# Post-norm attention and ternary FFN layer: the first row's first quad of scores moved ahead by a step, and where raw FFN weights wait

## The chip, the cores and the metric

The kernel runs on one core of a Trainium2 chip. The metric is device time in microseconds (us) of one execution. Three runs of the kernel before gave 1080.48, 1075.93 and 1077.56 us; their median is 1077.56 us.

## The reference

For 16 rows (batch entries) of 512 tokens and 256 features, in float32:

```
qkv = x @ Wqkv + bqkv                      # 16 heads of 16 features
scores = q . k / 16, keys of the own block of 128 tokens and of the two beside it
attn = softmax(where(|kpos - qpos| <= 128, scores, -1e30))
x1 = layernorm(x + (attn @ v) @ Wout + bout)
gamma = mean(|W|);  Wq = clip(round(W / (gamma + 1e-5)), -1, 1)     # for W1 and W2
out = layernorm(x1 + relu(x1 @ Wq1.T + b1) @ Wq2.T + b2)
```

The layer norms have no gain or shift. So the FFN weights have to be brought to -1, 0 or 1 on the chip, with thresholds that need the mean of all their absolute values.

## The kernel before, in words

**Tiling.** The 16 heads are taken in four quads of four heads (v or vq = 0 to 3). A quad's scores and its maxima are each worked out in 12 units: i = 0 to 11, head i // 3, and u = i % 3 says which key blocks (or query blocks). Two units of every three are one matmul of 384 columns, the third is two matmuls of 256 columns (`BLOCKS`, `PCOL`). Products that need float32 accuracy are done from a high and a low part ("hi" and "lo"), which for queries and keys are stacked along the partitions in `q_stack` and `k_stack` by DMAs.

**One quad's chain.** `max_scores` (TensorE, L567) fills a PSUM bank `mx`; `row_max` (VectorE, L1061) adds the band and takes the maximum; `neg_max` (L1069, L1072) negates the 16 maxima and splits them in two; step "nmt" transposes them (TensorE, L631; ScalarE copies them out, L938), and SP's DMA `maxima` (L489) writes them as two more rows of `q_stack`. Then `scores` (TensorE, L549) fills a bank `st` with scores that already have their maximum subtracted, `exp` (ScalarE, L895) turns them into `probs`, `mask` (GpSimd, L1285 and L1289; two per quad, after exp unit 5 and 11) zeroes what lies outside the band, and step "pv" (TensorE, L641) multiplies them by the values. There are two `st` and two `mx` banks: a score unit waits for the exponential of the unit two before it, a max unit for the row maximum of the unit two before it.

**Order.** Every engine runs its own instruction list in order. `steps` calls the body for at = -2, -1, 0, ... 16. At step `at`, row `at` has its attention, row at - 1 its FFN, and rows at + 1 and at + 2 are prepared. Each step has four parts v = 0 to 3, each a list `SIDE[v]` of side work, into which `WOVEN[v]` puts 12 score units and 12 max units. The scores are those of quad v of this row, the maxima those two quads ahead (`max_quad`): quads 2 and 3 of this row, then quads 0 and 1 of the next. At at = -1 there are no scores; `first_maxima` puts quad 0's maxima in v = 2 (among the projection "vp") and quad 1's maxima in v = 3: units 0 and 1 at "xr", then the transpose "nmt" of quad 0's maxima, then units 2 to 11 at "pv". In step 0, part v = 0 has no other work of TensorE than the "nmt" of quad 1, quad 0's scores and quad 2's maxima, since row 0 has no row before it. Part v = 1 begins with the projection "qk" (0) of row 1 (L592).

**SP's queue.** `TRANSFERS` is the order in which SP issues, in each step, the stack DMAs of a quad (six, L449), the `maxima` DMA after part v's "nmt", the columns of x, the residual x (into `y`, L482) and the stores. SP waits in that order. At at = -1 the order comes to: x, stack 0, stack 1, maxima (3) (which is quad 0's), stack 2; stack 3 follows as the first of step 0. `scores` of quad 0 waits for quad 0's maxima in `q_stack` and for stack 2.

**Raw weights.** The FFN weights come in raw and are quantised by GpSimd (`quantise`, L1299, L1300, L1303) in eight chunks of 512 columns. Chunks 0 to 3 (W2) and 4 and 5 (half of W1) lie in the second half of `probs`, which quad 1's exponentials will overwrite, chunks 6 and 7 in `x1`. The comparison "below" goes through the tile `oT_x1T_lo`. Chunks 0 to 2 are quantised at at = -1 (`other_weights`), 3 to 5 at the head of step 0 ahead of quad 0's masks, 6 and 7 after the two masks of quad 1. The first exponential of quad 1 waits for six chunks, and the first "ot" and "x1" on ScalarE and VectorE and the first "f1" on TensorE for all eight.

Of the kernel before, what the change touches and what calls it, by code (L numbers as in the profile page):

```python
# [27 lines left out]
B, S, D = 16, 512, 256  # L28
H, DH, W = 16, 16, 128
FF = 1024  # L30
NB = S // W
KC = D // P
# [42 lines left out]

TRANSFERS = (('stack', 3), ('maxima', 0), ('x', 0), ('stack', 0), ('maxima', 1), ('stack', 1), ('residual', 0), ('maxima', 2), ('maxima', 3), ('stack', 2), ('store', 0), ('store', 1))

LAG = {"ln1": 3, "ln2": 0, "qk": 0, "ut": 0, "ot": 1, "x1t": 0, "f1": 0, "op": 0, "f2": 0}
N_PAIRS = 2
WARM_END = {"ut": 3, "ot": 4, "op": 6, "x1t": 12}  # L80
# [67 lines left out]
def first_maxima(v):  # L148

    steps = {2: [(("f1", 1), range(N_MAX)), ("vp", range(N_MAX, UNITS))], 3: [("xr", range(N_MAX)), ("pv", range(N_MAX, UNITS))]}  # L150
    units = dict(steps.get(v, []))
    return [[(2 * u, "max", u) for u in units.get(s, ())] for s in SIDE[v]]


def stages(at):
# [67 lines left out]
def postln_layer(nc, xT, x, wqkv, bqk, bv, wout, bout, w1T, b1, w2T, b2, out):  # L223
    ctx = ExitStack()
    with ctx:
# [65 lines left out]
        WQRAW = PRF[0][:, 0:KC * 3 * D].rearrange("p (c n) -> p c n", c=KC)  # L291
        W2RAW = PRF[1][:, 0:FC * D]
        WORAW = PRF[1][:, FC * D:FC * D + KC * D]
        W1RAW = [X1[:, :, :].rearrange(FLAT), PRF[1][:, FC * D + KC * D:FC * D + KC * D + FF]]
        B1RAW = O[:, 0:2, :].rearrange(FLAT)


        def chunk(n):

            if n < 4:  # L300
                return W2RAW[:, S * n:S * n + S], W2Q[:, 2 * n:2 * n + 2, :].rearrange(FLAT), 1
            k, at = int(n < CHUNKS_IN_PROBS), S * (n % 2)
            return W1RAW[k][:, at:at + S], W1Q[:, k, at:at + S], 0

        CHUNKS, CHUNKS_IN_PROBS = 8, 6

        s_wq = sem("wqkv_in")
        s_w1 = sem("w1_in")
# [105 lines left out]
        @block.sync  # L414
        def _(sp):

            sp.dma_start(WQRAW, wqkv.rearrange("(c p) n -> p c n", p=P)).then_inc(s_wq, 16)

            def more_weights():
                sp.dma_start(WORAW.rearrange("p (c n) -> p c n", c=KC), wout.rearrange("(c p) n -> p c n", p=P)) \  # L420
                    .then_inc(s_wo, 16)
                sp.dma_start(W2RAW.rearrange("p (c n) -> p c n", n=D), w2T.rearrange("(c p) n -> p c n", p=P)) \
                    .then_inc(s_w2, 16)
                for k in range(KC):
                    sp.dma_start(W1RAW[k], w1T[P * k:P * k + P]).then_inc(s_w1, 16)
                sp.wait_ge(s_const, CONSTANTS)
                for row in (0, 32, 64, 96):
                    blocks = b1.rearrange("(c i n) -> i c n", i=2, n=P)[row // 64:row // 64 + 1]
                    sp.dma_start(B1RAW[row:row + 1].rearrange("a (c n) -> a c n", n=P), blocks).then_inc(s_b1, 16)
                sp.dma_start(BOUT[:, :], bout[None, :].to_broadcast([P, D])).then_inc(s_b2, 16)  # L430
                sp.dma_start(B2[:, :], b2[None, :].to_broadcast([P, D])).then_inc(s_b2, 16)

            def stack(r, v, first):


                c, ih = v // 2, v % 2
                if not first:
                    sp.wait_ge(s_stf, 12 * (4 * r - 4 + v) + 12)
                half = slice(64 * ih, 64 * ih + 64)
                heads = slice(4 * ih, 4 * ih + 4)  # L440
                for part, done in ((0, s_qkh), (1, s_qkl)):
                    sp.wait_ge(done, 4 * r + 2 * c + 2)
                    for dst, j, terms in ((SQ, 2 * c, (0, 1, 0)), (SK, 2 * c + 1, (0, 0, 1))):
                        if first and v == 0 and dst is SK:
                            continue
                        for t in range(3):
                            if terms[t] == part:
                                rows = slice(64 * c + 16 * t, 64 * c + 16 * t + 16)
                                sp.dma_start(dst[rows, heads, :].bitcast(F32), QK[j][part][half, :].bitcast(F32)) \  # L449
                                    .then_inc(s_stk[v], 16)  # L450

            def step(b, at):
                attn, post, nxt, nxt2 = stages(at)
                for kind, v in TRANSFERS:
                    if kind == "x" and nxt2:
                        x_columns(b + 2)
                        if at == -2:
                            sp.dma_start(BQK[:, :], bqk).then_inc(s_small, 16)
                            sp.dma_start(BV[:, :], bv).then_inc(s_small, 16)
                            more_weights()  # L460
                    elif kind == "stack" and v == 3 and attn:
                        stack(b, 3, at == 0)
                    elif kind == "stack" and v < 3 and nxt:
                        stack(b + 1, v, at == -1)
                    elif kind == "store" and post:
                        store(b, v, slice(2 * v, 2 * v + 2) if at == B else slice(v, v + 3, 2))
                    elif kind == "residual" and attn:
                        residual(b)
                    elif kind == "maxima" and row_of(v, "nmt", at) is not None:
                        dr, vq = row_of(v, "nmt", at)  # L470
                        maxima(b + dr, vq)

            def x_columns(r):
                if r > 0:
                    sp.wait_ge(s_xl, r)
                sp.dma_start(XRAW[:, :, :], xT[r:r + 1].rearrange("a (c p) t -> p (a c) t", p=P)).then_inc(s_x, 16)

            def residual(r):
                if r > 0:
                    for t in range(TB):  # L480
                        sp.wait_ge(*x1_done(r - 1, t))
                sp.dma_start(Y[:, :, :], x[r:r + 1].rearrange("a (t p) d -> p (a t) d", p=P)).then_inc(s_xr, 16)  # L482

            def maxima(r, vq):

                q, c, ih = 4 * r + vq, vq // 2, vq % 2
                sp.wait_ge(s_nmt, q + 1)
                rows = SQ[64 * c + 48:64 * c + 50, 4 * ih:4 * ih + 4, :].bitcast(F32)
                sp.dma_start(rows.rearrange("a g (n q) -> a (g n) q", n=NB), NMT[:, vq % 2].bitcast(F32)) \  # L489
                    .then_inc(s_nmin[vq], 16)  # L490

            def store(b, h, tiles):
                sp.wait_ge(s_o, 4 * (b - 1) + 2 * h + 2)
                sp.dma_start(out[b - 1:b].rearrange("a (t p) d -> p (a t) d", p=P)[:, tiles, :],
                             X1[:, tiles, :]).then_inc(s_out, 16)

            steps(step)
            sp.wait_ge(s_out, 32 * B)


        @block.tensor
        def _(pe):
# [238 lines left out]
            def step(b, at):  # L741
                attn = stages(at)[0]
                for v in range(QUADS):
                    q = max_quad(v, at)
                    for step, woven in zip(SIDE[v], first_maxima(v) if at == -1 else WOVEN[v]):
                        places = [0]

                        def units(until):
                            for place, kind, i in woven:
                                if places[0] <= place < until:  # L750
                                    if kind == "scores" and attn:
                                        scores(b, v, i, at)
                                    elif kind == "max" and q is not None:
                                        max_scores(b + q[0], q[1], i, at == -1)
# [97 lines left out]
        def _(act):  # L852
# [45 lines left out]
            def side_work(v, step, b, dr, vq, at):  # L898
# [47 lines left out]
                    act.activation(U[:, :], PG[:, 2 * k, :], ACT.Identity).then_inc(s_u, 1)  # L946
                elif name == "ot":
                    act.wait_ge(s_otf, 2 * r + 2)
                    if first:
                        act.wait_ge(s_quant, CHUNKS)  # L950
                    else:
                        act.wait_ge(s_f1f, FC * r)
                    for i in range(KC):
                        act.activation(OT[0][:, i, :], PG[:, 2 * k + i, :], ACT.Identity, bias=BV[:, i:i + 1]) \
# [23 lines left out]
            def step(b, at):  # L978
                attn = stages(at)[0]
                for v in range(QUADS):  # L980
# [3 lines left out]
                    for step, woven in zip(SIDE[v], WOVEN[v]):  # L984
# [2 lines left out]
                        if row is not None and before:  # L987
                            side_work(v, step, b, *row, at)
                        for _, kind, i in woven:
                            if kind == "scores" and attn:  # L990
                                exp(b, v, i, at)
                        if row is not None and not before:
                            side_work(v, step, b, *row, at)
                if at == B:
# [31 lines left out]
        def _(dve):  # L1026
# [48 lines left out]
            def side_work(v, step, b, dr, vq, at):  # L1075
# [26 lines left out]
                        on = dve.tensor_tensor(o, ut[:, i, :, :, 0:DH], sums.to_broadcast([P, TB, 2, DH]), ALU.mult)  # L1102
                    on.then_inc(s_on, 1)
                elif name == "ot":
                    if first:
                        dve.wait_ge(s_quant, CHUNKS)
                    for i in range(KC):
                        dve.wait_ge(s_oth, 2 * r + i + 1)
                        dve.scalar_tensor_tensor(OT[1][:, i, :], PG[:, 2 * k + i, :], BV[:, i:i + 1],
# [146 lines left out]
        def _(pool):  # L1256
# [36 lines left out]
            def quantise(n):  # L1293

                raw, ternary, i = chunk(n)
                if n > 1:
                    pool.wait_ge(s_quant, n - 1)
                below = OT[1][:, n % 2, :]
                pool.tensor_scalar(below, raw, THR[:, 2 + i:3 + i], None, ALU.is_lt).then_inc(s_below, 1)  # L1299
                pool.tensor_scalar(ternary, raw, THR[:, i:i + 1], None, ALU.is_gt).then_inc(s_above, 1)  # L1300
                pool.wait_ge(s_below, n + 1)
# [3 lines left out]
            def other_weights():  # L1305
# [10 lines left out]
                                       ALU.subtract).then_inc(s_b1l, 1)  # L1316
                pool.wait_ge(s_b1l, 2)
                pool.wait_ge(s_thr, 1)
                for n in range(3):
                    quantise(n)  # L1320

            quantised = [CHUNKS_IN_PROBS]


            def v_in_place(r, v, first):
# [48 lines left out]
            def step(b, at):  # L1374
                attn = stages(at)[0]
                for v in range(QUADS):
                    if at == -1 and v == 0:
                        other_weights()
                    if v == 0 and attn:
                        for vq in range(3):  # L1380
                            v_in_place(b, vq, at == 0)
                        if at == 0:
                            for n in range(3, CHUNKS_IN_PROBS):
                                quantise(n)
                    for step, woven in zip(SIDE[v], WOVEN[v]):
                        if attn:
                            for _, kind, i in woven:
                                if kind == "scores" and i in (5, 11):
                                    mask(b, v, i // 3)
                                    if at == 0 and v > 0 and quantised[0] < CHUNKS:  # L1390
                                        quantise(quantised[0])
                                        quantised[0] += 1
                            if v == 0 and step == "pv":
# [61 lines left out]
```

## Time and profile before

| | |
|---|---|
| median of 3 runs | 1077.56 us |
| the profiled execution | 1080.47 us |
| its span, first to last instruction | 1078.7 us |
| TensorE, VectorE busy | 92%, 78% |
| ScalarE, GpSimd busy | 57%, 53% |
| mean granted clock of TensorE | 0.969 |

Busy shares are of the span. Each row of the batch takes some 60 us, all alike from row 1 on; what the change touches lies in the first 110 us. PE is TensorE's matmuls, PEld its weight loads, DVE VectorE, ACT ScalarE, POOL GpSimd, SP the engine that issues most DMAs. PEclk 1.00 is 2.4 GHz and 0.50 is 1.2 GHz. Unit numbers are not in the trace; they are counted from the order of the instructions.

### The profile page before, as it was taken

Reading aid. Unit: us, or ns where it says so; the run is one execution under the profiler, and the core shown is the slowest. Engines: PE = TensorE matmul, PEld = TensorE weight load, DVE = VectorE, ACT = ScalarE, POOL = GpSimd, SP = SyncE. Lnnn points to the kernel's source line nnn. Section 1 sums busy time; section 2 is a strip of 40 time slices with the busy share of each in tenths; the row PEclk is TensorE's granted clock in tenths of the full one; section 3 lists DMA queues with packets and bytes.
Section 4 is the critical chain, followed back from the end, with each engine's and each line's share of the span. In section 5 each row is a group of like instructions: output and inputs, shape, how many; then the busy total and the mean of one; then the engine's idle time right before and its main releaser. Section 6 shows DMA issues by size and latency. Waiting matters only on the chain.

```text
span 1078.7 us, 29877 instructions
## 1 busy us (share of the span) xinstructions
PE 996.8 (92%) x11270; PEld 782.0 (72%) x11270; DVE 845.2 (78%) x2966; ACT 620.2 (57%) x1273; POOL 570.2 (53%) x913
## 2 busy tenths in 40 slices
PE   6898999999999999999999999999999999999897
PEld 5675777777777777777767777786777778687677
DVE  3775888879788887978888787988878798887535
ACT  4244665746566574756657474765747475564632
POOL 3975356374655537465554646454464645445352
PEclk8577999999999999999999999999999999999999
DMA  9554336546354545626454652645365364435000
GB/s 222 64 82 72 57 57 95 81 74 94 55 91 66 96 70 81 99 43 97 66 96 63 94 87 49 100 65 96 56 100 80 57 96 68 73 52 81 22 21 20
DMA packets 57023, 81.90 MB, mean 76 GB/s; under 512 B 7712, under 2 KB 27696, under 8 KB 56880
## 3 DMA queue, kind: packets, MB, share of 16 engines
q1 hardware_dynamic: 56640, 79.60, 46.8%
q8 instruction: 90, 1.47, 0.7%
q10 hardware_dynamic: 240, 0.39, 0.3%
q14 instruction: 53, 0.43, 0.2%
HBM read 20.20 MB, written 8.39 MB: 26 GB/s over the span
## 4 chain that ended last, share of the span: by engine, by line
PE 61%; DVE 13%; ACT 12%; issue 6%; POOL 4%; DMA 2%; SPq 1%; DVEq 0%; POOLq 0%; ACTq 0%
PE shared L592 26%; PE shared L641 11%; PE st L549 8%; PE mx L567 6%; DVE mx L1061 6%; ACT probs L895 4%; PE shared L521 2%; ACT x L963 2%; ACT u L946 2%; DVE hid_lo L1147 2%; PE shared L654 2%; ACT oT_x1T_hi L969 2%; PE shared L612 1%; POOL probs L1285 1%; POOL probs L1289 1%
## 5 line engine op out<-in xcount | busy, mean ns | idle before, releaser
L1061 DVE CUSTOM_DVE_ANT_0 mx<-mx,band 128x384 f32<-128x384 f32 (+1 forms) x1024 | 478.9, 518 | 150.5 <-PE mx L567 145.4
L895 ACT ACTIVATE probs<-st 128x384 f32<-128x384 f32 (+1 forms) x768 | 365.1, 526 | 169.8 <-PE st L549 168.1
L1285 POOL TENSOR_SCALAR_AFFINE_SELECT probs<-probs 128x512 f32<-128x512 f32 (+1 forms) x256 | 127.8, 524 | 407.0 <-ACT probs L895 407.0
L567 PE MATMUL mx<-k_stack,q_stack 48*128 48x384 f32 (+1 forms) x1024 | 271.7, 347 | 8.5 <-DMA q_stack<-qk_lo 4.9
L549 PE MATMUL st<-q_stack,k_stack 50*128 50x384 f32 (+1 forms) x1024 | 245.1, 334 | 7.8 <-ACT probs L895 3.8
L549 PEld LDWEIGHTS st<-q_stack,k_stack 50*128 50x128 f32 x1024 | 167.7, 189 | 58.9 <-issue 29.8
L567 PEld LDWEIGHTS mx<-k_stack,q_stack 48*128 48x128 f32 x1024 | 171.8, 193 | 31.1 <-DVE rmax L1061 19.2
L641 PE MATMUL shared<-probs,v_aug 128*32 128x384 f32 (+1 forms) x2048 | 164.2, 444 | 9.4 <-POOL probs L1289 7.2
L1061 DVE DVE_READ_ACCUMULATOR2_ANT rmax<- 128x1 f32 x1024 | 144.9, 141 | 0.0
L592 PE MATMUL shared<-w2q,hid_hi 64*128 64x256 f32 x960 | 137.0, 289 | 0.0
L641 PEld LDWEIGHTS shared<-probs,v_aug 128*32 128x32 f32 x2048 | 90.5, 111 | 55.8 <-issue 17.7
L592 PE MATMUL shared<-w2q,hid_lo 64*128 64x256 f32 x960 | 129.2, 278 | 0.0
L1289 POOL TENSOR_SCALAR_AFFINE_SELECT probs<-probs 128x512 f32<-128x512 f32 (+1 forms) x256 | 127.7, 523 | 0.0
L592 PEld LDWEIGHTS shared<-w2q,hid_lo 64*128 64x128 f32 x960 | 114.9, 185 | 0.0
L592 PEld LDWEIGHTS shared<-w2q,hid_hi 64*128 64x128 f32 x960 | 113.3, 185 | 0.4
L592 PE MATMUL shared<-oT_x1T_hi,w1q 64*128 64x512 f32 x480 | 104.0, 398 | 0.0
L592 PE MATMUL shared<-oT_x1T_lo,w1q 64*128 64x512 f32 x480 | 102.4, 394 | 0.0
L946 ACT ACTIVATE u<-shared 128x512 f32<-128x512 f32 x64 | 37.9, 593 | 102.1 <-PE shared L641 102.0
L521 PE MATMUL shared<-wqkv_hi 64*128 64x512 f32 x516 | 86.6, 417 | 3.9 <-DVE qk_lo L1088 3.8
L1147 DVE SCALAR_TENSOR_TENSOR hid_lo<-shared,hid_hi 128x512 fp32r<-128x512 f32 x120 | 77.0, 682 | 16.1 <-ACT hid_hi L976 16.1
L1371 POOL TENSOR_SCALAR x<-x,ln_mv,ln_rstd 128x256 f32<-128x256 f32 x60 | 73.5, 1230 | 3.2
L976 ACT ACTIVATE hid_hi<-shared 128x512 fp32r<-128x512 f32 x120 | 65.2, 596 | 13.9 <-PE shared L592 12.7
(165 smaller groups left out, 1935.7 us busy)
## 6 DMA issues: line engine op xcount, KB each, us to landing
q_stack<-qk_hi SPq DMA_DIRECT2D x128, 128.0 KB, 4.0
k_stack<-qk_hi SPq DMA_DIRECT2D x126, 128.0 KB, 4.9
x_raw<-in_xT SPq DMA_DIRECT2D x16, 512.0 KB, 6.0
q_stack<-qk_lo SPq DMA_DIRECT2D x64, 128.0 KB, 5.6
y<-in_x SPq DMA_DIRECT2D x16, 512.0 KB, 6.3
out<-x SPq DMA_DIRECT2D x32, 256.0 KB, 2.4
k_stack<-qk_lo SPq DMA_DIRECT2D x63, 128.0 KB, 5.8
probs<-in_w2T SPq DMA_DIRECT2D x1, 1024.0 KB, 7.5
```

The lines of the kernel that those rows point to most:

```text
L521: pe.matmul(out[i][:, 0:width], WQKV[0][rows, 0, 0:P], WQKV[0][rows, 1, 0:width], start=True, stop=True)
L549: mm = pe.matmul(PST[i % N_SCORE][:, col:col + n], SK[rows, hd, W * m:W * m + W], SQ[rows, hd, q0:q0 + n], start=True, stop=True)
L567: mm = pe.matmul(PMX[i % N_MAX][:, col:col + n], SQ[rows, hd, W * m:W * m + W], SK[rows, hd, k0:k0 + n], start=True, stop=True)
L592: mm = pe.matmul(out[k][:, cols], lhs(rows), rhs(rows), start=(swap == 0 and n == 0 and bias is None), stop=(swap == 1 and n == count - 1) ...
L641: mm = pe.matmul(out[0][32 * g:32 * g + 32, q0:q0 + width], VAUG[:, vq, m, g, :], PR[:, vq % 2, g // 2, lo:lo + width], start=(m == 0), st ...
L895: act.activation(PR[:, v % 2, g // 2, lo:lo + n], PST[i % N_SCORE][:, 0:n], ACT.Exp, scale=SCALE) \
L976: act.activation(HID[0][:, f, :], PG[:, 2 * k + i, :], ACT.Relu).then_inc(s_hh, 1)
L1061: mx = dve.tensor_tensor_reduce(ps, ps, band, 1.0, -3e38, ALU.add, ALU.max, RMAX[:, g, m:m + 1])
L1147: dve.scalar_tensor_tensor(HID[1][:, f, :], PG[:, 2 * k + i, :], 0.0, HID[0][:, f, :].bitcast(F32), ALU.max, ALU.subtract).then_inc(s_hl, 1)
L1285: pool.affine_select(out=pr_before, in_=pr_before, compare_op=ALU.is_ge, fill=0.0, base=0, pattern=[[0, n], [1, W]], channel_multiplier=-1)
L1289: last = pool.affine_select(out=pr_after, in_=pr_after, compare_op=ALU.is_ge, fill=0.0, base=0, pattern=[[0, n], [-1, W]], channel_multipl ...
L1371: pool.tensor_scalar(X1[:, t, :], X1[:, t, :], MV2[:, t, 0:1], RS2[:, t:t + 1], ALU.subtract, ALU.mult).then_inc(s_o, 1)
```

## The change

- At at = -1, part v = 3, two of quad 0's score units are issued on TensorE ahead of each of quad 1's max units 6 to 11. ScalarE does the 12 exponentials right after it has copied out quad 0's maxima. In step 0, part v = 0 no scores and exponentials are left, only quad 2's maxima.
- SP issues at at = -1 the DMAs of stack 2 ahead of quad 0's maxima (`FIRST_TRANSFERS`).
- Raw chunks 4 and 5 come into `y`. The first residual DMA waits for six quantised chunks. "below" goes through `hid_lo`, and two waits for all chunks at the first "ot" go.
- The chunks are quantised otherwise: 0 to 2 as before; none at the head of step 0; 3 after quad 0's second mask, 4 and 5 after quad 1's two masks, 6 and 7 after quad 2's two masks. The first exponential of quad 1 waits for four chunks.

```diff
+FIRST_TRANSFERS = TRANSFERS[:8] + (('stack', 2),) + TRANSFERS[8:9] + TRANSFERS[10:]
...
-    return [[(2 * u, "max", u) for u in units.get(s, ())] for s in SIDE[v]]
+    def with_scores(u):
+        early = range(2 * (u - UNITS // 2), 2 * (u - UNITS // 2) + 2) if v == 3 and 2 * u >= UNITS else ()
+        return [(2 * u, "scores", i) for i in early] + [(2 * u, "max", u)]
+
+    return [sum((with_scores(u) for u in units.get(s, ())), []) for s in SIDE[v]]
...
-        W1RAW = [X1[:, :, :].rearrange(FLAT), PRF[1][:, FC * D + KC * D:FC * D + KC * D + FF]]
+        W1RAW = [X1[:, :, :].rearrange(FLAT), Y[:, :, :].rearrange(FLAT)]
...
-        CHUNKS, CHUNKS_IN_PROBS = 8, 6
+        FIRST_CHUNKS, CHUNKS_IN_PROBS, CHUNKS_IN_Y, CHUNKS = 3, 4, 6, 8
...
             def residual(r):
-                if r > 0:
+                if r == 0:
+                    sp.wait_ge(s_quant, CHUNKS_IN_Y)
+                else:
...
-                                    if kind == "scores" and attn:
+                                    if kind == "scores" and at == -1:
+                                        scores(b + 1, 0, i, at + 1)
+                                    elif kind == "scores" and attn and (at, v) != (0, 0):
                                         scores(b, v, i, at)
...
+                        if at == -1 and v == 3 and step == "nmt":
+                            for i in range(UNITS):
+                                exp(b + 1, 0, i, at + 1)
...
-                below = OT[1][:, n % 2, :]
+                below = HID[1][:, n % 2, :]
...
-                        if at == 0:
-                            for n in range(3, CHUNKS_IN_PROBS):
-                                quantise(n)
...
-                                    if at == 0 and v > 0 and quantised[0] < CHUNKS:
+                                    if at == 0 and (v, i) != (0, 5) and quantised[0] < CHUNKS:
```

## Rows read from the trace of the kernel before

**Rows 1.** The page: busy time, and the chain that ended last.
```profile
PE 996.8 (92%) x11270; PEld 782.0 (72%) x11270; DVE 845.2 (78%) x2966; ACT 620.2 (57%) x1273; POOL 570.2 (53%) x913
...
PE 61%; DVE 13%; ACT 12%; issue 6%; POOL 4%; DMA 2%; SPq 1%; DVEq 0%; POOLq 0%; ACTq 0%
```

**Rows 2.** Stretches: busy per engine (instructions), TensorE's clock, DMA share, GB/s.
```profile
core 0: us, PE busy (x) PEld busy (x) DVE busy (x) ACT busy (x) POOL busy (x), PEclk, DMA share, GB/s
36.60:46.90 10.30, 8.30 (x21) 4.32 (x20) 9.06 (x34) 1.54 (x4) 10.15 (x10) 0.50 0.63 83
46.90:49.70 2.80, 1.56 (x6) 0.81 (x6) 0.35 (x3) 0.44 (x2) 2.65 (x3) 0.50 1.13 111
49.70:58.80 9.10, 8.56 (x37) 6.15 (x37) 7.96 (x32) 5.86 (x12) 8.80 (x8) 0.50 0.76 109
```

**Rows 3.** Timeline of VectorE: start, duration, instruction [idle before <- releaser].
```profile
42.23 0.57 DVE L1061 CUSTOM_DVE_ANT_0 mx<-mx,band 128x384 f32<-128x384 f32 x1
...
47.13 0.18 DVE L1072 SCALAR_TENSOR_TENSOR neg_max<-rmax,neg_max 128x16 f32<-128x16 f32 x1
49.70 0.57 DVE L1061 CUSTOM_DVE_ANT_0 mx<-mx,band 128x384 f32<-128x384 f32 x1 [2.39 <-PE mx L567]
```

**Rows 4.** Timeline of SP's DMA issues, and landing times of q_stack's DMAs, 36 to 52.
```profile
38.72 0.66 SPq L489 DMA_DIRECT2D q_stack<-neg_maxT  x1
...
42.58 0.60 SPq L449 DMA_DIRECT2D k_stack<-qk_lo  x1
...
76.92 0.59 SPq L482 DMA_DIRECT2D y<-in_x  x1
...
DMA to landing us min/median/max: 3.3/6.1/8.8
```

**Rows 5.** Timeline of TensorE.
```profile
37.78 0.61 PE L631 MATMUL shared<-identity,neg_max 128*32 128x128 f32 x2 [0.82 <-DVE neg_max L1072]
38.35 1.20 PE L567 MATMUL mx<-k_stack,q_stack 48*128 48x256 f32 x3
...
47.36 0.63 PE L631 MATMUL shared<-identity,neg_max 128*32 128x128 f32 x2 [0.53 <-DVE neg_max L1072]
48.77 0.66 PE L549 MATMUL st<-q_stack,k_stack 50*128 50x384 f32 x1 [0.78 <-DMA k_stack<-qk_lo]
...
50.07 0.58 PE L549 MATMUL st<-q_stack,k_stack 50*128 50x256 f32 x1 [0.20 <-ACT probs L895]
51.55 0.69 PE L549 MATMUL st<-q_stack,k_stack 50*128 50x384 f32 x1
...
52.81 0.69 PE L549 MATMUL st<-q_stack,k_stack 50*128 50x384 f32 x1
...
57.32 0.76 PE L592 MATMUL shared<-xT_hi,wqkv_hi 64*128 64x512 f32 x1
```

**Rows 6.** Stretches by TensorE's clock, columns as in Rows 2.
```profile
30.00:32.00 2.00, 2.00 (x17) 1.83 (x15) 1.51 (x9) 0.00 (x0) 1.85 (x2) 0.50 0.00 0
...
62.00:64.00 2.00, 2.00 (x26) 1.47 (x26) 0.17 (x2) 0.71 (x2) 0.47 (x2) 0.87 0.00 0
```

**Rows 7.** Timeline of GpSimd.
```profile
68.55 1.00 POOL L1285 TENSOR_SCALAR_AFFINE_SELECT probs<-probs 128x512 f32<-128x512 f32 x2 [6.08 <-ACT probs L895]
...
70.48 1.57 POOL L1299 TENSOR_SCALAR oT_x1T_lo<-x,abs_sums_thresholds 128x512 fp32r<-128x512 f32 x1
...
74.97 1.00 POOL L1285 TENSOR_SCALAR_AFFINE_SELECT probs<-probs 128x512 f32<-128x512 f32 x2
...
82.07 1.00 POOL L1285 TENSOR_SCALAR_AFFINE_SELECT probs<-probs 128x512 f32<-128x512 f32 x2 [0.62 <-ACT probs L895]
...
88.29 1.00 POOL L1285 TENSOR_SCALAR_AFFINE_SELECT probs<-probs 128x512 f32<-128x512 f32 x2 [4.27 <-ACT probs L895]
```

**Rows 8.** Timeline of TensorE: the products of quads 1 and 2 with the values.
```profile
84.35 2.32 PE L641 MATMUL shared<-probs,v_aug 128*32 128x256 f32 x29
...
92.15 4.47 PE L641 MATMUL shared<-probs,v_aug 128*32 128x256 f32 x29
```

More of the change, by code:

```diff
@@ L301, in chunk @@
                 return W2RAW[:, S * n:S * n + S], W2Q[:, 2 * n:2 * n + 2, :].rearrange(FLAT), 1
-            k, at = int(n < CHUNKS_IN_PROBS), S * (n % 2)
+            k, at = int(n < CHUNKS_IN_Y), S * (n % 2)
             return W1RAW[k][:, at:at + S], W1Q[:, k, at:at + S], 0
-        CHUNKS, CHUNKS_IN_PROBS = 8, 6
+        FIRST_CHUNKS, CHUNKS_IN_PROBS, CHUNKS_IN_Y, CHUNKS = 3, 4, 6, 8
         s_wq = sem("wqkv_in")
@@ L453, in step @@
                 attn, post, nxt, nxt2 = stages(at)
-                for kind, v in TRANSFERS:
+                for kind, v in FIRST_TRANSFERS if at == -1 else TRANSFERS:
                     if kind == "x" and nxt2:
@@ L948, in side_work @@
                     act.wait_ge(s_otf, 2 * r + 2)
-                    if first:
-                        act.wait_ge(s_quant, CHUNKS)
-                    else:
+                    if not first:
                         act.wait_ge(s_f1f, FC * r)
@@ L989, in step @@
                         for _, kind, i in woven:
-                            if kind == "scores" and attn:
+                            if kind == "scores" and attn and (at, v) != (0, 0):
                                 exp(b, v, i, at)
+                        if at == -1 and v == 3 and step == "nmt":
+                            for i in range(UNITS):
+                                exp(b + 1, 0, i, at + 1)
                         if row is not None and not before:
@@ L1104, in side_work @@
                 elif name == "ot":
-                    if first:
-                        dve.wait_ge(s_quant, CHUNKS)
                     for i in range(KC):
@@ L1318, in other_weights @@
                 pool.wait_ge(s_thr, 1)
-                for n in range(3):
+                for n in range(FIRST_CHUNKS):
                     quantise(n)
-            quantised = [CHUNKS_IN_PROBS]
+            quantised = [FIRST_CHUNKS]
             def v_in_place(r, v, first):
```

## The prediction
> **What bounds the kernel now.** I read the page first: TensorE is busy 92% of the span and holds 61% of the chain that ended last [rows 1]. All that the change touches happens once, in the first 110 us; the other fifteen rows run the same lists as before and are only pushed earlier or later. So the question is when step 0 hands TensorE over to row 1's projection "qk" (0), the first work that does not depend on quads 0 to 2. Before, that was at 57.32 us [rows 5].
>
> Then I cut the time around the change into stretches [rows 2]. From 36.6 to 46.9 quad 1's maxima run, and VectorE is busy 9.06 of 10.3 us: this stretch is VectorE's. From 49.7 to 58.8 quad 0's scores and quad 2's maxima run together, TensorE busy 8.56 and VectorE 7.96 of 9.1 us: the two are nearly level. Between them VectorE stands still 2.39 us [rows 3]. The timeline of TensorE shows what it waits for: the transpose at 47.36 is out, and the first score at 48.77 is released by the last DMA of stack 2 [rows 5], issued at 42.58 behind quad 0's maxima [rows 4].
>
> **The change, part by part.**
>
> *The wait for stack 2 goes.* Its DMAs are issued some 15 us earlier. What comes next is the way through the transpose: at 37.78 a transpose of the same kind was followed by a max unit 0.57 us later [rows 5]. From 47.36 that gives a max unit at 47.93; with 0.66 us for one matmul of 384 columns [rows 5] VectorE starts at 48.6 and not at 49.70. Gain 1.1 us.
>
> *Quad 0's scores go into the second half of quad 1's maxima.* They need quad 0's maxima in `q_stack`. That DMA is issued at 38.72 [rows 4]; its landing is not in the trace. The shortest landing of the larger DMAs into the same tile at that time is 3.3 us, the longest 8.8 (on a crowded queue, which this DMA no longer meets); the lower bound is the end of its issue, 0.66. I take 3.3, the row of an empty queue: the scores can start at 42.0. Unit 6 of the maxima, behind which the first half ends, was taken by VectorE at 42.23 [rows 3], so TensorE got to it at about 41.5, and 0.5 us are lost at once. With a landing below 2.8 us nothing is lost.
>
> Two banks hold the scores, so a unit starts when the exponential two before it is done. In the stretch with the same clock a unit of 2 x 256 columns took its bank from 50.07 to 51.55, 1.48 us, and one of 384 from 51.55 to 52.81, 1.26 us [rows 5]. Bank 0 has units 0, 2, 4, 6, 8, 10, and units 2 and 8 are of 2 x 256: unit 10 starts 3 x 1.26 + 2 x 1.48 = 6.7 us after unit 0, at 48.7; unit 11 some 0.35 later, max unit 11 after it at 49.5, and VectorE ends it at 50.9. The lower bound is TensorE's own rate: 24 units in 8.56 us busy [rows 2] are 0.36 us each, and 12 score and 6 max units from 41.5 are then done at 47.9; that leaves the maxima some 1.4 us late. Before, VectorE ended them at 46.9. So the six max units take 4.0 us longer (1.4 to 4.0, more if the DMA lands later). I take 4.0, since a wait for the exponential shows between the scores of the nearest row.
>
> *Quad 2's maxima are left alone in step 0.* It is tempting to count the 12 removed score units (12 x 0.36 = 4.3 us of TensorE) as a gain. But VectorE has the same 16 reductions and accumulator reads to do, and in quad 1's stretch, without scores beside it, it needed 10.3 us with its first units early, that is the same pace: 9.1 us for quad 2 with the scores [rows 2]. I take the gain as 0; the bound below is 9.1 - 7.96 = 1.1 us, VectorE's idle time in the stretch. ScalarE's exponentials (5.86 us busy [rows 2]) bind neither there nor in their new place.
>
> So quad 2's maxima end 4.0 - 1.1 = 2.9 us later, and so does the start of "qk" (0): 57.3 becomes 60.2.
>
> *The clock.* The clock was 0.50, 1.2 GHz, until about 62.5 (0.87 in the stretch from 62 to 64 [rows 6]), after some 5 us of dense projection. If it rises at the same time, the 2.9 us of dense work that is still to do runs at twice the pace and costs half, and the delay is 1.45 us. If it rises as much later as the projection starts later, the delay stays 2.9. I take the middle, 2.2 us.
>
> A row of the trace and the Trainium skill differ on this clock. In the stretch from 30 to 32, as in those around it, TensorE was busy 2.00 of 2 us with projection and maxima, and the clock stayed at 0.50 [rows 6]. The page "TensorE: Matmul & The Clock Gate", section "Part 1: The HAM clock gate", has sustained matmul activity release the throttle. By that rule the fuller stretch after the change could bring the clock up before 50; by the row, a full busy time is not enough for it. I follow the row; the rule's outcome is the second rival.
>
> *GpSimd.* One quantisation is 4.5 us (70.48 to 74.97), two masks 1.93 us (68.55 to 70.48) [rows 7]. Before, three quantisations stood ahead of quad 0's masks; now its masks come first, and chunk 3 after them. Quad 0's masks were ready before TensorE asked for them, so this gains nothing; chunk 3 ends about 57, ahead of quad 1's exponentials. Later the chain is fuller. With everything 2.9 us late: quad 1's first masks 71.4 to 73.4, chunk 4 to 77.9, second masks to 79.9, chunk 5 to 84.4, quad 2's first masks (before at 82.07 [rows 7], so due at 85.0) to 86.9, chunk 6 to 91.4, second masks (before at 88.29, due at 91.2) to 93.3. TensorE asks for them at about 92.0 + 2.9 = 94.9 [rows 8]. So it costs 0, with 1.6 us of cover, and what hides it is the wait of the masks for the exponentials. If the cover is gone, the cost is at most one quantisation less the cover, 4.5 - 1.6 = 2.9 us. Chunk 7, the low part of row 2's columns and the biased residual come behind, and are asked for by steps of row 1.
>
> *The new wait on SP.* The residual DMA waits for six chunks, until 84.4, and was issued at 76.92 [rows 4]. Behind it on SP stands the `maxima` DMA of quad 3, issued at 85 or later before; 0 us, with under a us of cover plus the 2.9 us by which that one is late as well.
>
> *Edits of one answer.* Other tiles for raw chunks and "below" cost 0: same instructions, same sizes. The two waits that go at "ot" were met long before; 0.
>
> Sum: +4.0 - 1.1 + 0 - 0.7 (clock) = +2.2 us. The profiled execution took 1080.47 us (span 1078.7), so one like it would take 1082.7. It stands 2.9 us above the median of the three runs, and I predict against that median: 1077.56 + 2.2 = 1079.8 us.
>
> **The rivals.**
>
> A: *the overlap works as meant* (18%). The maxima land early and TensorE packs the 18 units at its own rate: +1.4 - 1.1, and quad 2's maxima lose some of their 1.1 us of idle time. With the clock's halving this is -0.5 to -1: about 1077 us. For it: TensorE has 2 of 10.3 us free in that stretch. Against it: two banks only.
>
> B: *the clock comes up early, or falls less often* (15%). If it is up before 50, "qk" (0) from 57.3 to 63.2 takes 3 us and not 5.9, and quad 2's maxima 8 us and not 9.1: +2.9 - 2.9 - 1.1 = about -1; and later, quad 2's product with the values took 4.47 us at the low clock where quad 1's took 2.32 [rows 8], and quad 3's took as long: another 2 to 4.3 us if those stretches run at 2.4 GHz. Time 1072 to 1076; the middle is 1074. The same dice can fall the other way: one more low stretch costs 2 us.
>
> C: *the quantisations get in the masks' way* (15%). GpSimd's chain has quad 2's second masks behind chunks 4, 5 and 6. From the point where they end after 94.9, TensorE waits for them at the product with the values, in order, with scores and maxima of the next part behind it. Price 2.9 us on top of 2.2, and with the first masks of quad 3 late behind chunk 7 up to 2 more: 1082.7 to 1084.7. For it: GpSimd has no gap left from 71 to 86. Against it: the exponentials bind by my sum.
>
> D: *the change does nothing that shows* (in the forecast's range): the wait moves from one DMA to another.
>
> **How the numbers follow.** Forecast 52%, A 18%, B 15%, C 15%. No change is told from a change here by 0.5%, 5.4 us: below 1072.2 or above 1082.9. Faster by that: the far end of B, 7%. Slower by that: most of C and late landings of quad 0's maxima, 13%. Same: 80%. The range for 8 in 10 goes from 1074.5 (the middle of B, and the spread of the runs before, 4.5 us) to 1084.5 (C).
>
> **What would show it.** Right: VectorE's gap at the change from quad 1's to quad 2's maxima under 1.8 us; quad 1's last max at 50 to 51; a stall of TensorE for quad 0's maxima of about 0.5 us; quad 2's stretch 9 us without scores; "qk" (0) at about 60. Wrong: a projection that starts before 58; TensorE's product of quad 2 released by GpSimd; a clock of 1.00 before 58. The prediction fails if row 1 starts earlier than before at the same clock.

## The result

The changed kernel took 1084.09 us (median of 9 runs, 1082.45 to 1084.97) and the kernel before, in the same rounds, 1080.48 us (9 runs, 1075.93 to 1081.51). The ratio is 1.0042, with a 95% interval of 1.0028 to 1.0056: the change costs 3 to 6 us, around 4.5. I had forecast 1079.8 us, +2.2 us on a base of 1077.56. The direction was right, and the size was half of the 4.5 us.

The changed kernel's profiled execution took 1083.39 us, 2.9 us more than that of before. On the page the busy times and the chain have hardly moved (TensorE 996.8 before, [rows 1]), so the time went into waiting:

```profile
span 1081.6 us, 29875 instructions
...
PE 997.2 (92%) x11270; PEld 781.2 (72%) x11270; DVE 845.3 (78%) x2966; ACT 619.6 (57%) x1273; POOL 568.7 (53%) x913
...
PE 61%; DVE 14%; ACT 11%; issue 6%; POOL 4%; DMA 2%; SPq 1%; DVEq 0%; POOLq 0%; ACTq 0%
```

The three stretches that answer to [rows 2] are quad 1's maxima, now with quad 0's scores, the gap, and quad 2's maxima, now alone. Columns as there.

```profile
37.30:51.40 14.10, 12.67 (x37) 8.08 (x37) 9.25 (x34) 7.55 (x16) 10.95 (x14) 0.50 0.44 59
51.40:53.80 2.40, 1.32 (x4) 0.68 (x4) 0.96 (x3) 0.27 (x1) 2.40 (x5) 0.50 0.00 0
53.80:63.00 9.20, 7.57 (x22) 4.76 (x23) 7.96 (x32) 0.00 (x0) 3.32 (x3) 0.50 0.22 59
```

The first stretch is 3.8 us longer, with 0.2 us more work on VectorE: VectorE no longer sets its length. The gap is 0.4 us shorter. The third is as long as before, 9.2 us against 9.1, with 7.96 us of VectorE in both: twelve score units less beside it gained nothing.

The cadence of the scores can be read from TensorE's timeline:

```profile
40.84 1.31 PE L576 MATMUL mx<-k_stack,q_stack 48*128 48x384 f32 x3 [0.55 <-DVE rmax L1073]
42.16 0.97 PE L558 MATMUL st<-q_stack,k_stack 50*128 50x384 f32 x2
42.93 0.52 PE L576 MATMUL mx<-k_stack,q_stack 48*128 48x384 f32 x1
43.45 1.11 PE L558 MATMUL st<-q_stack,k_stack 50*128 50x256 f32 x3
...
44.93 1.17 PE L558 MATMUL st<-q_stack,k_stack 50*128 50x384 f32 x3
...
46.33 1.15 PE L558 MATMUL st<-q_stack,k_stack 50*128 50x384 f32 x2
...
47.60 1.14 PE L558 MATMUL st<-q_stack,k_stack 50*128 50x256 f32 x3
...
48.95 1.17 PE L558 MATMUL st<-q_stack,k_stack 50*128 50x384 f32 x3
...
52.48 0.64 PE L640 MATMUL shared<-identity,neg_max 128*32 128x128 f32 x2 [1.08 <-DVE neg_max L1084]
```

From 42.16, the start of score unit 0, to 48.95, the start of unit 10, are 6.8 us; I had worked out 6.7. From pair to pair it is 1.27 to 1.48 us, and between two pairs of scores VectorE gets one max unit. What the scores wait for is the exponential that frees their bank, and VectorE waits for them in turn. First the waits that were found from 36 to 63 (in all, times, longest), then ScalarE and VectorE in that stretch:

```profile
PEld st L558 <- ACT probs L906: 1.9, 5, 0.6
PEld st L558 <- issue: 0.3, 1, 0.3
```

```profile
44.28 0.98 ACT L906 ACTIVATE probs<-st 128x512 f32<-128x512 f32 x2 [0.50 <-PE st L558]
45.66 1.08 ACT L906 ACTIVATE probs<-st 128x384 f32<-128x384 f32 x2 [0.40 <-PE st L558]
```

```profile
44.92 0.57 DVE L1073 CUSTOM_DVE_ANT_0 mx<-mx,band 128x384 f32<-128x384 f32 x1 [0.81 <-PE mx L576]
46.57 0.43 DVE L1073 CUSTOM_DVE_ANT_0 mx<-mx,band 128x256 f32<-128x256 f32 x1 [1.02 <-PE mx L576]
```

Along the time line the two profiled executions compare as follows (start times from the timelines; the last column takes off that the first row maximum starts 0.68 us later, which e4 below gives no reason to put down to the change).

| | before | after | later | less 0.68 |
|---|---|---|---|---|
| first row maximum, VectorE | 25.06 | 25.74 | 0.68 | 0 |
| quad 1's maxima negated (low part) | 47.13 | 51.87 | 4.74 | 4.06 |
| quad 2's maxima negated | 59.33 | 63.35 | 4.02 | 3.34 |
| "qk" (0) of row 1 | 57.32 | 61.51 | 4.19 | 3.51 |
| quad 0's product copied out (`u`) | 65.83 | 69.60 | 3.77 | 3.09 |
| quad 3's maxima negated | 76.09 | 79.85 | 3.76 | 3.08 |
| row 1's quad 1 maxima negated | 103.74 | 107.58 | 3.84 | 3.16 |
| the last `u` | 1043.20 | 1046.07 | 2.87 | 2.19 |

All is lost by 52 us, some is won back by 70, and from there the delay is handed on through the rows. It shrinks by 0.9 us on the way to the last `u`, little by little and without a place that the traces name.

The clock rose later, in the stretch from 64 to 66 and not from 62 to 64 [rows 6]; the busy time of TensorE was full before it in both:

```profile
62.00:64.00 2.00, 2.00 (x12) 1.92 (x11) 1.45 (x8) 0.00 (x0) 0.00 (x0) 0.50 0.00 0
64.00:66.00 2.00, 2.00 (x13) 1.96 (x13) 0.78 (x3) 0.87 (x2) 0.00 (x0) 0.54 0.00 0
66.00:68.00 2.00, 2.00 (x27) 1.38 (x28) 0.57 (x3) 0.93 (x2) 0.00 (x0) 1.00 0.00 0
```

### The profile page after: what moved, and what is told of

Its sections match the earlier page's. It is cut to its first block, busy times and chain, and to the rows that moved or that the text cites. A ratio compares the mean times of both kernels' runs of the same rounds, so it can differ in the third digit from the quotient of the medians.

```text
span 1081.6 us, 29875 instructions
## 1 busy us (share of the span) xinstructions
PE 997.2 (92%) x11270; PEld 781.2 (72%) x11270; DVE 845.3 (78%) x2966; ACT 619.6 (57%) x1273; POOL 568.7 (53%) x913
## 4 chain that ended last, share of the span: by engine, by line
PE 61%; DVE 14%; ACT 11%; issue 6%; POOL 4%; DMA 2%; SPq 1%; DVEq 0%; POOLq 0%; ACTq 0%
PE shared L601 26%; PE shared L650 11%; PE st L558 8%; PE mx L576 6%; DVE mx L1073 6%; ACT probs L906 4%; PE shared L530 2%; ACT x L972 2%; ACT u L957 2%; DVE hid_lo L1157 2%; PE shared L663 2%; ACT oT_x1T_hi L978 2%; PE shared L621 1%; POOL probs L1295 1%; POOL probs L1299 1%
```

## The experiments

All had 12 timed runs, with 29 or 35 runs of the kernel before on the same chip. Their theory: the loss is the stretch in which two score banks hold back quad 1's maxima; the rest is small.

### e1_stack2_early: one part of the change alone

```diff
+FIRST_TRANSFERS = TRANSFERS[:8] + (('stack', 2),) + TRANSFERS[8:9] + TRANSFERS[10:]
...
-                for kind, v in TRANSFERS:
+                for kind, v in FIRST_TRANSFERS if at == -1 else TRANSFERS:
```

> The kernel before, with one part of the change: stack 2's DMAs ahead of quad 0's maxima on SP. Theory (the change is a stretched stage of maxima, partly paid for by the wait that goes): without early scores the wait for stack 2 goes and quad 2's maxima start 1 us earlier, but the first maxima of quad 0 start 0.7 us later, because stack 2's DMAs share the DMA engines with the last of stack 0: 0 to -1 us against before. Rival 1 (the first maxima start late by chance of the profiled run): -1.1 us, first maxima at 24.6 as before. Rival 2 (the change is slower because of stack 2's place): slower by 1 us or more.

Measured: 1079.82 us, before 1079.82; ratio 1.0000 (0.9986 to 1.0014). In the profile the first row maximum started at 26.13, and counted from it everything is earlier: quad 3's maxima are negated 50.16 us later and not 51.03 as in the kernel before. So the wait that goes is worth 0.9 us in the trace, in the range of "0 to -1" that was expected, and too little to show in the time.

### e2_chunks_only: the other part alone

The changed kernel with scores and transfers as before:

```diff
-        early = range(2 * (u - UNITS // 2), 2 * (u - UNITS // 2) + 2) if v == 3 and 2 * u >= UNITS else ()
+        early = ()
...
-                for kind, v in FIRST_TRANSFERS if at == -1 else TRANSFERS:
+                for kind, v in TRANSFERS:
...
-                                    elif kind == "scores" and attn and (at, v) != (0, 0):
+                                    elif kind == "scores" and attn:
...
```

> The changed kernel with scores and transfers as before: only the raw chunks' tile, the order of quantisations and masks, and the residual's wait are changed. Theory (GpSimd has cover): within 0.5 us of before. Rival (fuller GpSimd costs: masks late at quads 2 and 3, or VectorE slowed by it): 1 to 3 us slower than before, the product of quad 2 released by GpSimd.

Measured: 1083.10 us, ratio 1.0029 (1.0014 to 1.0044). The theory failed here, and the rival named the wrong place. ScalarE's timeline shows it:

```profile
58.86 0.60 ACT L906 ACTIVATE probs<-st 128x512 f32<-128x512 f32 x1 [0.42 <-PE st L558]
66.07 0.87 ACT L906 ACTIVATE probs<-st 128x384 f32<-128x384 f32 x2 [6.61 <-POOL w2q L1313]
```

Quad 1's first exponential waits 6.61 us for GpSimd's chunk 3. That chunk now stands behind quad 0's second mask; with scores as before this mask comes at 59.5, and chunk 3 ends at 66.0. In the changed kernel the scores are early, the mask is done at 52.7 and chunk 3 at 57.3, ahead of the exponentials at 64.91. So e2's 3 us belong to e2 and not to the change: the two parts lean on each other, and e2 does not measure the second part in its place.

### e3_six_early: half as many early scores

```diff
-        early = range(2 * (u - UNITS // 2), 2 * (u - UNITS // 2) + 2) if v == 3 and 2 * u >= UNITS else ()
+        early = (u - UNITS // 2,) if v == 3 and 2 * u >= UNITS else ()
...
-                                    elif kind == "scores" and attn and (at, v) != (0, 0):
+                                    elif kind == "scores" and attn and ((at, v) != (0, 0) or i >= UNITS // 2):
...
```

> The changed kernel with one early score unit ahead of each of quad 1's max units 6 to 11, not two; score units 6 to 11 stay in step 0, part 0. Theory (two score units per max unit make the two score banks the bound, 1.3 us per max unit against VectorE's 0.76): with one, TensorE needs 0.72 us per max unit, the stretch grows by 0.5 to 1 us for the start and not by 3.8, and quad 2's stretch stays at 9.1: 2.5 to 3.5 us faster than the changed kernel, within 1 us of before. Rival (the delay comes from elsewhere: clock, GpSimd, DMA): as slow as the changed kernel.

Measured: 1083.43 us, ratio 1.0037 (1.0019 to 1.0055), as slow as the changed kernel. Taken alone this would speak for the rival. But its trace shows the same wait as e2's, since the last six scores are late again:

```profile
65.93 0.87 ACT L906 ACTIVATE probs<-st 128x384 f32<-128x384 f32 x2 [6.62 <-POOL w2q L1313]
```

### e7_six_chunk3 and e8_chunks_chunk3: the same two without that wait

```diff
+                        if at == 0:
+                            quantise(3)
...
-            quantised = [FIRST_CHUNKS]
+            quantised = [FIRST_CHUNKS + 1]
...
-                                    if at == 0 and (v, i) != (0, 5) and quantised[0] < CHUNKS:
+                                    if at == 0 and v > 0 and quantised[0] < CHUNKS:
```

> The kernel e3 (six early score units) with chunk 3 quantised at the head of step 0, ahead of the masks, as before. Theory (e3 lost its gain since quad 1's exponentials waited 6.6 us for chunk 3, which stood behind quad 0's second mask): that wait goes, and the kernel is within 1 us of before, 3 us faster than the changed one. Rival (early scores cost as such, however many there are per max unit): as slow as the changed kernel.

> The kernel e2 (raw chunks' part alone) with chunk 3 quantised at the head of step 0. Theory (e2's 3 us were the same wait for chunk 3, which the changed kernel does not have, since its scores are early): within 0.7 us of before. Rival (the fuller GpSimd, the residual's wait or the new tile cost by themselves): 2 us or more slower than before, as e2.

Measured: e7 1078.63 us against 1079.43, ratio 0.9985 (0.9965 to 1.0005); e8 1081.78, ratio 0.9997 (0.9977 to 1.0017). e7 is as its theory has it, 5 us faster than e3. e8 is less clear: its ratio is level with before, within 2.5 us faster and 1.8 us slower, but its median is 2.35 us above that of before, and its runs spread from 1075.17 to 1083.64. So it does not decide between theory and rival. e12 below, the same with stack 2 early, is level with before by both.

e7 shows what two score units per max unit cost. Its stretch on TensorE and on VectorE:

```profile
41.41 0.65 PE L558 MATMUL st<-q_stack,k_stack 50*128 50x384 f32 x1
41.86 0.52 PE L576 MATMUL mx<-k_stack,q_stack 48*128 48x384 f32 x1
42.18 0.52 PE L558 MATMUL st<-q_stack,k_stack 50*128 50x384 f32 x1
42.50 0.59 PE L576 MATMUL mx<-k_stack,q_stack 48*128 48x384 f32 x1
...
45.40 0.63 PE L558 MATMUL st<-q_stack,k_stack 50*128 50x256 f32 x2
```

```profile
42.42 0.56 DVE L1073 CUSTOM_DVE_ANT_0 mx<-mx,band 128x384 f32<-128x384 f32 x1
43.13 0.57 DVE L1073 CUSTOM_DVE_ANT_0 mx<-mx,band 128x384 f32<-128x384 f32 x1
...
48.00 0.17 DVE L1084 SCALAR_TENSOR_TENSOR neg_max<-rmax,neg_max 128x16 f32<-128x16 f32 x1
```

A score unit and a max unit take 0.8 us together, and from the first score to the last row maximum VectorE never waits for more than 0.26 us. From the first row maximum (25.03) to quad 1's negation are 22.97 us; before it was 22.07, in the changed kernel 26.13. So six early units cost 0.9 us and twelve 4.1. A part of both is the first negation, which took 0.57 us in e7, 0.35 in the changed kernel and 0.17 before; up to its start they cost 0.5 and 3.9. The step lies where the score banks' 1.3 us per max unit pass VectorE's 0.76 (9.1 us for twelve).

Against the changed kernel e7 differs in two things, the number of early scores and chunk 3's place. Chunk 3 early without the other was not run; that its place costs the changed kernel nothing is read from the trace, where chunk 3 ends 7.6 us before ScalarE starts quad 1's exponentials (57.3 and 64.9).

### e12_chunk3_stack2: e7 without its early scores

Against e7:

```diff
-        early = (u - UNITS // 2,) if v == 3 and 2 * u >= UNITS else ()
+        early = ()
...
```

> The kernel e8 (raw chunks' part with chunk 3 early, no early scores) with stack 2 early: e7 without its six early score units. Theory (the six units are nearly free but win nothing either, since quad 2's stretch is VectorE's with them or without): within 1 us of e7 and of before. Rival (the six early units are what makes e7 faster): e7 is faster than this by 1.5 us or more.

Measured: 1079.23 us, before 1079.27; ratio 1.0003 (0.9986 to 1.0019). By the medians as the theory has it, within 1 us of e7 and of before. By the ratios e7 is ahead by 1.9 us, each known to some 2 us, so the time does not rule the rival out. The traces speak against it: quad 3's maxima are negated 50.11 us after the first row maximum in e7 and 50.27 in e12. The early scores win next to nothing, since the stretch they leave is VectorE's.

### e4_stack2_held: is stack 0 held up by stack 2?

```diff
+                        if at == -1 and v == 2:
+                            sp.wait_ge(s_mxf, 1)
```

> The changed kernel, SP waiting before stack 2 until quad 0's first max unit is done. Theory (0.7 us of the delay is stack 0 landing later, since stack 2 is issued right behind): first maxima at 24.6 and 0.7 us faster than the changed kernel. Rival (chance): no difference, first maxima at 24.6 or 25.3 in both.

Measured: 1083.97 us, ratio 1.0033 (1.0019 to 1.0046), no gain on the changed kernel that shows; 0.7 us is less than these intervals can tell. SP issued stack 2 at 26.41 and not at 21.80, and the first row maximum (some 0.5 us behind TensorE's first max unit, of which the text above speaks) started at 26.41 as well, no earlier than the 25.74 of the changed kernel. So nothing speaks for the theory. In kernels with stack 2 where it was before, that start was 25.06 (before), 26.33 (e2) and 25.95 (e8); with it early 25.74 (changed kernel), 26.13 (e1), 26.12 (e3), 25.63 (e6), 25.03 (e7) and 27.04 (e12). It moves by 2 us from one profiled execution to the next, in both orders.

### e6_mask_held: VectorE's small instructions beside a mask

In the changed kernel the two instructions `neg_max` of quad 1 took 0.35 and 0.55 us, with GpSimd's mask running from 50.82 to 52.75. The first fence is the changed kernel's VectorE, the second e6's.

```diff
+                if b == 0 and v == 0 and g == 3:
+                    pool.wait_ge(s_nm, 2)
```

> The changed kernel, GpSimd waiting ahead of quad 0's second mask until quad 1's maxima are negated. Theory (the two small VectorE instructions neg_max took 0.35 and 0.55 us there and not 0.17 and 0.18 because GpSimd's mask ran at the same time): 0.17 and 0.18 us, quad 2's maxima start 0.6 us earlier, 0.6 us faster than the changed kernel. Rival (they are slow for another reason): as long as in the changed kernel, no gain.

```profile
51.49 0.35 DVE L1081 TENSOR_SCALAR neg_max<-rmax 128x16 fp32r<-128x16 f32 x1
51.87 0.55 DVE L1084 SCALAR_TENSOR_TENSOR neg_max<-rmax,neg_max 128x16 f32<-128x16 f32 x1
53.88 0.57 DVE L1073 CUSTOM_DVE_ANT_0 mx<-mx,band 128x384 f32<-128x384 f32 x1 [1.45 <-PE mx L576]
```

```profile
51.35 0.17 DVE L1081 TENSOR_SCALAR neg_max<-rmax 128x16 fp32r<-128x16 f32 x1
51.56 0.17 DVE L1084 SCALAR_TENSOR_TENSOR neg_max<-rmax,neg_max 128x16 f32<-128x16 f32 x1
53.18 0.57 DVE L1073 CUSTOM_DVE_ANT_0 mx<-mx,band 128x384 f32<-128x384 f32 x1 [1.45 <-PE mx L576]
```

Measured: 1083.68 us, ratio 1.0021 (1.0001 to 1.0042), 0.4 us below the changed kernel's median, in the direction expected and not told apart by time. In the trace it is shown: 0.17 and 0.17 us with GpSimd still, 0.56 us less than in the changed kernel, and the gap between quad 1's and quad 2's maxima is 1.9 us (51.31 to 53.18) and not 2.4.

The same masks stood beside quad 2's negations in the kernel before and no longer do. So the change gets 0.33 us back there:

```profile
58.95 0.35 DVE L1069 TENSOR_SCALAR neg_max<-rmax 128x16 fp32r<-128x16 f32 x1
59.33 0.32 DVE L1072 SCALAR_TENSOR_TENSOR neg_max<-rmax,neg_max 128x16 f32<-128x16 f32 x1
```

```profile
63.14 0.17 DVE L1081 TENSOR_SCALAR neg_max<-rmax 128x16 fp32r<-128x16 f32 x1
63.35 0.17 DVE L1084 SCALAR_TENSOR_TENSOR neg_max<-rmax,neg_max 128x16 f32<-128x16 f32 x1
```

### e5_warm_gap and e9_six_warm: the low clock at the head

Both add to TensorE's first gap (e5 on top of e1, e9 of e7):

```diff
+                if first and v == 0 and i == 0:
+                    warm([PST[0], PST[1]], 20)
```

> The kernel e1 (before, with stack 2 early) and 20 pairs of matmuls of 512 columns, whose results nobody reads, on TensorE ahead of quad 0's first max unit, where it stands still for 4.9 us and after which the clock fell to 0.50 until 62. Theory (the low clock of this stretch is a price of its own, which the change does not touch): if the clock stays at 1.00 through the projection behind it, that is 2 us shorter, the maxima 1 us per quad, and the projection of row 1 3 us: 4 to 7 us faster than before. Rival (the clock falls anyway, since the maxima leave TensorE too thin): within 1 us of e1, the clock at 0.50 from about 36 at the latest.

> The kernel e7 (six early score units, chunk 3 early) with the 20 pairs of matmuls of e5 in TensorE's first gap. Theory (e5's 2 us in quad 0's maxima and e7's gain lie in different stretches): they add: quad 0's maxima end 9.8 us after the first and not 12.0, the kernel is 2 to 3 us faster than before. Rival (what is won at the head is given back by the time the clock rises again for row 1's projection): as fast as e7.

Measured: e5 1077.77 against 1079.43, ratio 0.9983 (0.9962 to 1.0004); e9 1078.06 against 1079.27, ratio 0.9986 (0.9970 to 1.0003). The clock of e5 and of e9 where it fell:

```profile
28.00:30.00 2.00, 2.00 (x18) 1.84 (x18) 1.98 (x9) 0.00 (x0) 2.00 (x2) 0.75 1.14 130
30.00:32.00 2.00, 2.00 (x17) 2.00 (x16) 1.57 (x7) 0.00 (x0) 1.85 (x3) 0.50 1.06 103
```

```profile
30.00:32.00 2.00, 1.86 (x19) 1.50 (x18) 1.98 (x9) 0.00 (x0) 1.90 (x2) 1.00 1.06 102
32.00:34.00 2.00, 1.59 (x10) 0.89 (x10) 1.90 (x9) 1.26 (x2) 2.00 (x2) 0.92 1.09 118
```

The clock stayed at 2.4 GHz through part (e5) or all (e9) of quad 0's maxima (low part negated 9.8 us after the first row maximum in e5, 8.8 in e9, 12.0 before), and fell in both before row 1's projection. That is 2 to 3 us at this place in the traces and 1 to 2 us in the medians, of which the intervals just reach no change. For e5 neither theory nor rival held whole. For e9 the rival's time held: by the medians it is 0.6 us faster than e7 and by the ratios level with it (0.9986 and 0.9985), though its trace is 3.3 us ahead of e7's when quad 3's maxima are negated (46.85 and 50.11 us after the first row maximum). e5, e9 and e7 have the lowest medians of this study; that any of them beats the kernel before is not shown.

### e11_filled: a full TensorE beside quad 2's maxima

The changed kernel, with

```diff
+                                        if at == 0 and v == 0 and i > 1:
+                                            warm(pair_free(PAIR[(0, "ut")], b), 1)
```

> The changed kernel with a pair of matmuls of 512 columns, whose results nobody reads, behind each of quad 2's max units 2 to 11 in step 0, part 0, where TensorE has only those maxima. Theory (part of the changed kernel's price is the clock, which rises only 4.3 us after the projection of row 1 has begun): with TensorE full, the clock is at 1.00 when that projection begins, it takes 3 us and not 5.5, and the kernel is 2 to 2.5 us faster than the changed one, 2 us slower than before. Rival (the maxima are so thin that the clock does not rise, and the added matmuls only get in their way): the clock rises where it did, same time as the changed kernel or 1 us slower.

Measured: 1083.14 us, ratio 1.0047 (1.0031 to 1.0064). The rival holds. In the stretches, columns as in [rows 2],

```profile
56.00:66.00 10.00, 10.00 (x45) 8.29 (x44) 6.72 (x28) 0.00 (x0) 1.28 (x1) 0.50 0.12 46
66.00:68.00 2.00, 2.00 (x14) 1.70 (x13) 1.14 (x4) 0.87 (x2) 0.00 (x0) 0.79 0.00 0
```

TensorE was busy without a gap from 56 on, the projection began at 62.5 (61.5 in the changed kernel), and the clock rose in the stretch from 66 to 68 (0.79), later than in the changed kernel. So a full busy time did not bring it up (with the reserve that the ends of matmuls are modelled in the profile, so that small pauses between them need not show). That this mix of matmuls leaves the clock low is shown; why it does stays open. The rule of the Trainium skill, page "TensorE: Matmul & The Clock Gate", section "Part 1: The HAM clock gate", that sustained matmul activity releases the throttle, does not agree with this row either, and the measurement decides.

## Why the prediction was right or wrong

The mechanism was right: the score banks stretch quad 1's maxima, and the wait for stack 2 pays a part of it. What failed are sizes. A term was missing (the masks' new place, put at 0, measured +0.55), two gains were taken too large (the wait for stack 2, -1.1 for -0.9; the clock, -0.7 for -0.4), and the base of 1077.56 us was 2 to 3 us low.

**Quad 0's scores in quad 1's maxima: +4.0.** Measured +3.9 up to the start of the first negation (46.92 before, 51.49 after, less 0.68). The bank loop was 6.8 us for 6.7. The scores began at 42.16, 2.7 us after the issue of quad 0's maxima at 39.45; I had taken 3.3, and no stall of TensorE for this DMA shows in the trace. e7 shows the mechanism by halving the early scores: 0.5 us.

**The wait for stack 2: -1.1.** e1 gives 0.9 for the wait by itself: from quad 1's low negation to quad 2's first row maximum it has 1.65 us (48.26 to 49.91), the kernel before 2.57 (47.13 to 49.70).

**The masks' new place: 0.** This step I did not have: GpSimd's mask, moved ahead, falls on the two instructions that negate quad 1's maxima and on which the transpose waits. They took 0.90 us together and 0.35 before, so it costs 0.55, of which 0.17 stands in the table's 4.06 and the rest in the gap behind it; e6 takes 0.56 away. I had costed the masks' new place at nothing since nobody waits for the masks, and not asked what runs beside them.

**Quad 2's maxima alone: 0.** Right, 9.2 us for 9.1; e12 and e7 say the same from the other side.

**The clock: -0.7.** At the projection the delay is 3.5 us, after it 3.1: the clock's share was -0.4. It rose about 3.3 us later in the trace (at 65.8 for 62.5, worked out from the means of the stretches and the two levels), and the projection began 4.2 us later. I took the middle of my range; it lay nearer to the end at which the clock follows the projection.

**GpSimd's quantisations, SP, tiles: 0.** Right for the changed kernel: quad 2's second masks ran from 92.10 to 94.02, the product began at 95.54. Chunk 3's place is the one thing among them that could cost, and it did in e2 and e3.

**The sum: +2.2.** By the trace it is +3.1: +3.9, +0.55 and -0.9 make the 3.5 at the projection, less 0.4 behind it. So 0.9 us were mis-sized, in the masks, the wait and the clock. The other part of the miss is the base. I took 1077.56, the median of three runs, and put the profiled execution 2.9 us above it. With 9 runs the median was 1080.48, with 29 to 35 runs of each later job 1079.3 to 1079.8: the profiled execution was an ordinary one, and the median of the three was low. The sum against its own time, 1082.7, missed the result by 1.4 us; the sum against the median missed it by 4.3.

**What is left.** The trace gives 3.1 from one execution of each kernel, the ratio 3 to 6 with 4.5 in the middle. e4, the changed kernel with a wait that gained nothing, measured 3.6 (ratio 1.0033), so chance may be enough for the other 1.4 us. The clock may have a part in it. The kernel before ran at a mean granted clock of 0.9696 over 70 of its runs, and its time goes with that mean: 1075.8 us at 0.974 (3 runs), 1080.0 at 0.969 (7), 1083.7 at 0.966 (5). The changed kernel's mean was 0.9676 over nine runs, with none above 0.970, and e4's 0.9677 over twelve. This can't be turned into microseconds, since the mean also counts the clock where TensorE stands still: in TensorE's gap before the first maxima the clock fell at about 21.4 in the changed kernel's trace and at 25.0, as the gap ended, in that of before. Whether the change lowers the mean, and what that costs, was not settled.

**The chances.** The ratio lies within 0.5%, which had 80%; the range ended at 1084.5 and held 1084.09 by 0.4 us. Rival A was wrong for the reason in the text against it. B's part of an early clock did not come, and e11 shows that a fuller TensorE does not bring it. C did not come in the changed kernel; something like its mechanism, a chunk ahead of somebody's need, was real in e2 and e3, one quad earlier than I had looked. Of the signs that I had named, quad 1's last maximum (ended 51.4, and 50.7 less 0.68), quad 2's stretch and "qk" (0) (61.5, and 60.8 less 0.68) came about as said. Two did not: VectorE's gap was 2.4 us and not under 1.8, of which the masks have some 0.5 us, and TensorE did not stall for quad 0's maxima.

## What to carry to other kernels

Work woven into a stage at two units per one unit of the bound engine must be held against its own loop, bank by bank, and not against the busy time of its engines; one unit per unit cost 0.5 us here and two 3.9. What an emptied stage gives back is read from the engine that bounds it, here nothing. When two parts of a change are tried apart, look in the trace whether a part alone makes a wait that the whole does not have; and take the base of a forecast from as many runs as its size asks for: three were 2 to 3 us off. And an engine that nobody waits for can still slow what runs beside it.

## What the runs showed of the hardware

Two VectorE instructions of 16 elements per partition took 0.17 us each with GpSimd idle (e6) and 0.32 to 0.55 with a GpSimd select running beside them (changed kernel at 51.49, kernel before at 58.95). Beside a quantisation on GpSimd the picture is mixed: 0.71 and 0.63 us in the kernel before at 36.26, but 0.17 and 0.18 at 46.92, where a quantisation ran from 46.33 to 47.89. What makes the difference was not looked into.

TensorE was busy 2.00 of 2 us for ten microseconds at 1.2 GHz, without the clock rising (e11 from 56 to 66, and the kernel before from 26 to 36). 20 pairs of matmuls in TensorE's first gap kept it at 2.4 GHz until about 29.0 in e5 (21.4 in e1, 25.0 in the kernel before) and 33.7 in e9 (23.0 in e7).
